# Routed tiles of an attention-and-experts kernel: turning x on TensorE, or by DMA transposes of 16-bit halves that ScalarE weaves together

## What is computed

```python
x = x + xattn(layernorm(x), k, bias, ctx, ctx, 8)   # long convolution, gated by ctx
x = x + ffn(layernorm(x))                           # mixture of experts

scores = softmax(xt @ Wg.T)                         # 16 experts in 4 groups
# the best 2 groups of a token are kept, and in them its best 4 experts
h = silu(einsum('td,eid->eti', xt, W1)) * einsum('td,eid->eti', xt, W3)   # 176 wide
expert_out = einsum('eti,edi->etd', h, W2)
y = einsum('etd,te->td', expert_out, combine)       # weighted sum of a token's experts
z = silu(xt @ Ws1.T) * (xt @ Ws3.T) @ Ws2.T         # shared expert, 352 wide
```

## Time and profile before

| what | value |
|---|---|
| three runs of the program | 396.35, 398.21, 399.11 us; median 398.21 |
| span of the profiled execution, first to last instruction | 395.4 us |
| PE busy | 384.7 us (97%) |
| PEld, DVE, POOL, ACT busy | 279.3, 244.1, 180.3, 162.9 us |
| DMA moved | 83.09 MB in 37,812 packets |

### The profile page before, as it was taken

How to read it: one execution, slowest core, us unless ns; L and a number is a source line. 1 busy time by engine, 2 the same in 40 slices (tenths; PEclk the granted TensorE clock), 3 DMA queues, 4 the chain that set the end, 5 groups by cost and what they waited for, 6 DMA issues and landing times.

```text
span 395.4 us, 9070 instructions
## 1 busy us (share of the span) xinstructions
PE 384.7 (97%) x2146; PEld 279.3 (71%) x2147; DVE 244.1 (62%) x676; ACT 162.9 (41%) x494; POOL 180.3 (46%) x225
## 2 busy tenths in 40 slices
PE   6999999999999999999999999999999999999996
PEld 6788888888888546555667675446767777777765
DVE  3577577987988465788735344443445464646466
ACT  5347656564564362101124333333333333334431
POOL 3254323337888573565553333333333333334333
PEclk9999999999999999999999999999999999999999
DMA  7974474368879996256376873334474737362737
GB/s 248 363 254 139 163 277 144 133 206 278 309 250 335 414 419 258 96 207 223 104 215 219 321 239 107 87 95 134 127 246 136 242 115 242 115 232 103 264 97 251
DMA packets 37812, 83.09 MB, mean 210 GB/s; under 512 B 5930, under 2 KB 25870, under 8 KB 35728
## 3 DMA queue, kind: packets, MB, share of 16 engines
q1 hardware_dynamic: 31248, 64.83, 49.1%
q0 software_dynamic: 6528, 17.84, 11.6%
HBM read 60.21 MB, written 23.48 MB: 212 GB/s over the span
## 4 chain that ended last, share of the span: by engine, by line
PE 79%; DVE 10%; DMA 4%; issue 2%; ACT 2%; SPq 1%; DVEq 1%; POOL 0%; POOLq 0%
PE heads L1382 18%; PE bank L1456 13%; PE heads L1271 11%; PE heads L1424 7%; PE heads L1273 5%; PE bank L1437 5%; PE heads L1392 4%; PE bank L1403 4%; PE bank L1285 3%; DVE kv L734 3%; PE heads L1374 3%; DMA toep<-toep_in 2%; PE bank L1448 2%; DVE prod L763 2%; DMA y_scratch<-toep,dest_i 2%
## 5 line engine op out<-in xcount | busy, mean ns | idle before, releaser
L716 POOL DMA_INDIRECT y_scratch<-toep,dest_i x72 | 71.8, 997 | 112.0 <-DVE dest_i L1131 96.0
L1382 PE MATMUL heads<-experts,toep 128*128 x256 | 86.6, 461 | 0.6 <-DVE toep L1089 0.5
L1271 PE MATMUL heads<-toep,kv 128*128 128x256 f32 x256 | 77.9, 386 | 1.9 <-DVE kv L734 0.8
L661 POOL DMA_INDIRECT rows_scratch<-rows,slot_i x64 | 63.3, 989 | 35.4 <-issue 19.5
L1456 PE MATMUL bank<-experts,toep 88*128 x256 | 66.2, 381 | 1.6 <-DVE toep L1096 1.6
L553 ACT ACTIVATE toep<-heads 128x176 f32<-128x176 f32 x72 | 22.8, 317 | 78.1 <-PE heads L1382 67.2
L1382 PEld LDWEIGHTS heads<-experts,toep 128*128 128x128 f32 x256 | 43.7, 190 | 14.8 <-issue 1.1
L1273 PEld LDWEIGHTS heads<-toep,kv 128*128 128x128 f32 x256 | 48.7, 190 | 6.5
L763 DVE TENSOR_TENSOR prod<-heads,ctx_rep 128x1024 f32<-128x1024 f32 x32 | 39.1, 1221 | 22.3 <-PE bank L1285 19.9
L1096 DVE COPY toep<-heads 88x256 f32<-88x256 f32 x72 | 30.2, 419 | 31.1 <-PE heads L1392 31.1
L1273 PE MATMUL heads<-toep,kv 128*128 128x128 f32 x256 | 49.2, 274 | 0.0
(11 more groups left out here) (240 smaller groups left out, 513.4 us busy)
## 6 DMA issues: line engine op xcount, KB each, us to landing
ctx_rep<-ctxr_in SPq DMA_DIRECT2D x16, 1024.0 KB, 5.0
experts<-experts_in SPq DMA_DIRECT2D x16, 608.0 KB
toep<-rows_scratch SPq DMA_DIRECT2D x56, 144.0 KB
prod<-y_scratch SPq DMA_DIRECT2D x5, 1024.0 KB, 5.5
rows_scratch<-pad_row SPq DMA_DIRECT2D x17, 144.0 KB, 1.8
ctx_tr<-ctxt_in SPq DMA_DIRECT2D x16, 128.0 KB
toep<-toep_in SPq DMA_DIRECT2D x4, 512.0 KB, 7.0
ctx_n<-ctx_in SPq DMA_DIRECT2D x16, 128.0 KB, 2.1
```

The source lines that it names most:

```text
L661: pool.indirect_dma_start(rows_d, bass.IndirectOffsetOnAxis(ap=slot_i[:, u, k:k + 1].bitcast(U32), axis=0), rows[:, u, :], None).then_inc( ...
L716: pool.indirect_dma_start(y_d, bass.IndirectOffsetOnAxis(ap=dest_i[b][:, 0:1].bitcast(U32), axis=0), y_sb[b], None, bounds_check=TOPK * TO ...
L1271: nc.tensor.matmul(y_ps[par][:, i, :], kv[:, q, 0, h * P:(h + 1) * P], toep[:, q * HH + h, :], start=True, stop=False)
L1382: last = nc.tensor.matmul(up_ps[p], x_tr[p][:, blk, :], up_w(e, blk), start=blk == 0, stop=blk == LB - 1)
```

## The change

The turned x no longer comes from TensorE. ACT writes a row in another form: after `norm2` has put the normalised row into a buffer `xn`, a new `split_row(u)` writes its 256 low and its 256 high 16-bit halves one behind the other into the same 1,024 bytes. POOL scatters the same 1,152 bytes a row, as 16-bit elements. SP loads a tile with a transposing DMA of these halves, which lands turned, and loads the last 32 words of each row (128 bytes) by a second, plain DMA. A mixed tile takes two of each. ACT's `src_tr` then weaves low and high halves into words of `x_tr`, two tiles ahead of `up`. SP reads four tiles' addresses with one load into four registers.

```diff
+            def turned(mem, at, lo, count):
+                return sp.dma_start_transpose(in_halves(mem).rearrange("p (r n) -> p r n", n=P)[:, :, lo:lo + count],
+                                              halves_d[bass.ds(at, count), 0:2 * L])
             def gather(t, b, before):
+                if b == 0:
+                    sp.load(row_of, tile_row[0:1, bass.ds(t, DEPTH)])
+                    if is_mixed(t):
+                        sp.load(also_of, other_row[0:1, t - MIXED0:t - MIXED0 + DEPTH])
+                at = sp.snap(row_of[b], min_val=0, max_val=E * REGION)
                 if not (isinstance(t, int) and t < DEPTH):
-                    sp.wait_ge(xtr_ps, t - (DEPTH - 1))
+                    sp.wait_ge(xtr_ready, t - (DEPTH - 1))
                     sp.wait_ge(taken, t - (DEPTH - 1))
-                at = sp.value_load(tile_row[0:1, bass.ds(t, 1)], min_val=0, max_val=E * REGION)
...
                 if is_mixed(t):
-                    sp.dma_start(xg[b][0:HALF], rows_d[bass.ds(at, HALF)]).then_inc(rows_in[b], 16)
-                    also = sp.value_load(other_row[0:1, t - MIXED0:t - MIXED0 + 1], min_val=0, max_val=E * REGION + HALF)
-                    sp.dma_start(xg[b][HALF:P], rows_d[bass.ds(also, HALF)]).then_inc(others_in[b], 16)
+                    turned(xg[b], at, 0, HALF).then_inc(rows_in[b], 16)
+                    also = sp.snap(also_of[b], min_val=0, max_val=E * REGION + HALF)
+                    turned(xg[b], also, HALF, HALF).then_inc(others_in[b], 16)
+                    sp.dma_start(xg[b][0:HALF, L:], rows_d[bass.ds(at, HALF), L:]).then_inc(gates_in[b], 16)
+                    sp.dma_start(xg[b][HALF:P, L:], rows_d[bass.ds(also, HALF), L:]).then_inc(other_gates[b], 16)
                 else:
-                    sp.dma_start(xg[b], rows_d[bass.ds(at, P)]).then_inc(rows_in[b], 16)
+                    turned(xg[b], at, 0, P).then_inc(rows_in[b], 16)
+                    sp.dma_start(xg[b][:, L:], rows_d[bass.ds(at, P), L:]).then_inc(gates_in[b], 16)
...
+            def split_row(u):
+                act.wait_ge(xn_ready, u + 1)
+                nc.scalar.activation(in_halves(rows[:, u, :]).rearrange("p (s l) -> p s l", s=2),
+                                     xn_of(u).bitcast(U16).rearrange("p (l s) -> p s l", s=2), ACT.Copy
+                                     ).then_inc(row_ready, 1)
...
-            def src_tr(w, p):
+            def src_tr(w, p, b, before):
                 if not (isinstance(w, int) and w < 2):
                     act.wait_ge(up_done, w - 1)
-                act.wait_ge(xtr_ps, w + 1)
-                nc.scalar.activation(x_tr[p], xt_ps[p], ACT.Copy).then_inc(xtr_ready, 1)
+                rows_landed(act, w, b, before)
+                nc.scalar.activation(x_tr[p].rearrange("p b n -> p (b n)").bitcast(U16).rearrange("p (n s) -> p n s", s=2),
+                                     in_halves(rows_of(w, b)).rearrange("p (s n) -> p n s", s=2), ACT.Copy
+                                     ).then_inc(xtr_ready, 1)
...
-            def routed_step(t, b, before):
+            def routed_step(w, b, before):
                 p = b % 2
-                silu(t, p)
-                if not (isinstance(t, int) and t == LIVE - 1):
-                    src_tr(t + 1, 1 - p)
-                if not (isinstance(t, int) and t < 2):
-                    store_y(t - 2, p, (b - 2) % DEPTH, before if b >= 2 else before - 1)
+                if not (isinstance(w, int) and w < 2):
+                    silu(w - 2, p)
+                src_tr(w, p, b, before)
+                if not (isinstance(w, int) and w < 4):
+                    store_y(w - 4, p, b, before - 1)
...
                 up(t, p, b)
-                if not (isinstance(t, int) and t == LIVE - 1):
-                    turn_x(t + 1, 1 - p, (b + 1) % DEPTH, before + 1 if b == DEPTH - 1 else before)
```

More of the change, by code:

```diff
@@ L221, in build @@
         s_up, s_silu, s_hid, s_down = sem("shared_up"), sem("shared_silu"), sem("shared_hid"), sem("shared_down")
-        rows_in = [sem(f"rows_in{b}") for b in range(DEPTH)]
-        xtr_ps, xtr_ready, up_done, silu_done, hid_ready, ht_done, htr_ready, dn_done = (
-            sem("xtr_ps"), sem("xtr_ready"), sem("up_done"), sem("silu_done"), sem("hid_ready"), sem("ht_done"),
+        rows_in, gates_in = ([sem(f"{n}_in{b}") for b in range(DEPTH)] for n in ("rows", "gates"))
+        xtr_ready, up_done, silu_done, hid_ready, ht_done, htr_ready, dn_done = (
+            sem("xtr_ready"), sem("up_done"), sem("silu_done"), sem("hid_ready"), sem("ht_done"),
             sem("htr_ready"), sem("dn_done"))
@@ L227, in build @@
         y_sent = [sem(f"y_sent{b}") for b in range(DEPTH)]
-        late_in = [sem(f"late_in{j}") for j in range(LATE)]
+        late_in, late_gates = ([sem(f"{n}{j}") for j in range(LATE)] for n in ("late_in", "late_gates"))
         sends_ready, unit_ps, unit_ready = sem("sends_ready"), sem("unit_ps"), sem("unit_ready")
@@ L232, in build @@
         other_in = [sem(f"other_in{g}") for g in range(MIXED)]
-        others_in = [sem(f"others_in{b}") for b in range(DEPTH)]
+        others_in, other_gates = ([sem(f"{n}{b}") for b in range(DEPTH)] for n in ("others_in", "other_gates"))
         added, finished = sem("added"), sem("finished")
@@ L237, in build, with xn_of @@
         block = ctx.enter_context(nc.Block())
+        def xn_of(u):
+            return spread[:] if u == UNITS - 1 else xn[:]
         def v_forward(q):
@@ L281, in rows_landed, with gates_landed @@
                 eng.wait_ge(rows_in[b], before * 16 + 16)
+            if is_mixed(t):
+                eng.wait_ge(others_in[b], (t - MIXED0) // DEPTH * 16 + 16)
+        def gates_landed(eng, t, b, before):
+            if is_late(t):
+                eng.wait_ge(late_gates[t - LIVE + LATE], 16)
+            else:
+                eng.wait_ge(gates_in[b], before * 16 + 16)
+            if is_mixed(t):
+                eng.wait_ge(other_gates[b], (t - MIXED0) // DEPTH * 16 + 16)
         def is_mixed(t):
@@ L408, in late_gather @@
                 t = LIVE - LATE + j
-                at = sp.value_load(tile_row[0:1, t:t + 1], min_val=0, max_val=E * REGION)
-                sp.dma_start(rows[:, UNITS - LATE + j, :], rows_d[bass.ds(at, P)]).then_inc(late_in[j], 16)
+                if j % DEPTH == 0:
+                    sp.load(late_of, tile_row[0:1, t:t + DEPTH])
+                at = sp.snap(late_of[j % DEPTH], min_val=0, max_val=E * REGION)
+                mem = rows[:, UNITS - LATE + j, :]
+                turned(mem, at, 0, P).then_inc(late_in[j], 16)
+                sp.dma_start(mem[:, L:], rows_d[bass.ds(at, P), L:]).then_inc(late_gates[j], 16)
             others_at = {5: (0,), 7: (1,), 8: (2,), 9: (3,), 10: (4,), 11: (5,), 13: (6,), 14: (7,)}
@@ L581, in _ @@
             copy_xn(UNITS - 1)
+            split_row(UNITS - 2)
             silu_shared(2)
+            split_row(UNITS - 1)
             copy_logits(UNITS - 1)
@@ L1114, in take @@
                 src = rows_of(t, b)
-                rows_landed(dve, t, b, before)
+                gates_landed(dve, t, b, before)
                 if not (isinstance(t, int) and t < DEPTH):
@@ L1303, in transpose_xn @@
                 for blk in range(LB):
-                    last = nc.tensor.transpose(xn_ps[:, blk, :], rows[:, u, blk * P:(blk + 1) * P], ident[:])
+                    last = nc.tensor.transpose(xn_ps[:, blk, :], xn_of(u)[:, blk * P:(blk + 1) * P], ident[:])
                 last.then_inc(xt_done, 1)
@@ L1393, in turn_h @@
                 last.then_inc(ht_done, 1)
-            def turn_x(t, p, b, before):
-                src = rows_of(t, b)
-                rows_landed(pe, t, b, before)
-                if is_mixed(t):
-                    pe.wait_ge(others_in[b], (t - MIXED0) // DEPTH * 16 + 16)
-                if not (isinstance(t, int) and t < 2):
-                    pe.wait_ge(xtr_ready, t - 1)
-                for blk in range(LB):
-                    last = nc.tensor.transpose(xt_ps[p][:, blk, :], src[:, blk * P:(blk + 1) * P], ident[:])
-                last.then_inc(xtr_ps, 1)
             def tile_lists():
@@ L1495, in _ @@
             pe.wait_ge(map_ready, 1)
-            turn_x(0, 0, 0, 0)
             down_shared(UNITS - 2)
```

35 lines of the change are left out of this document (22 added, 13 removed).

## The result

| | time, us (median, runs) | ratio to before, 95% | span of the profiled execution | granted clock |
|---|---|---|---|---|
| before | 397.67 (396.35 to 399.11, 4) | 1 | 395.4 | 1.00 |
| after | 439.41 (438.88 to 441.21, 4) | 1.105 [1.102, 1.108] | 437.6 | 0.965 |

The forecast was 407 with a range of 384 to 426: the side was right and so was the place, the size was not.

A forecast was written before the change was run, and what follows sets the result against it. SP's queue was to replace TensorE as the bound: 27.2 us lost on SP less 18.3 gained from turn_x gives +8.9, so 404.3 on the span and 407 on the median, range 384 to 426.

The forecast's parts named there:

- The place and the mechanism: SP's queue becomes the bound: late loads delay ACT's weave and TensorE's up; SP hardly waits for taken in tiles 16 to 63.
- p: A transposing load's time on SP with its preparation: taken as 1.27 us, bounds 0.43 and 5.1, break-even 1.15.
- SP's price of a tile: SP's work for a plain tile: 1.27 + 0.43 + 0.1 for waits = 1.8 us.
- the eight late loads: Extra loads on SP, four in tiles 24 to 31 and four in 32 to 39, priced at 1.7 us each.
- Address loads: On SP, one load of four addresses, once in four tiles, taken at 0.3 us.
- TensorE's need as predicted: TensorE's pace without turn_x: 2.27 us for a plain tile and 2.54 for a mixed one.
- the 2.0 us of lead: Tiles 8 to 15: loads may run four tiles ahead, of which about 2.0 us is lead, leaving a loss of 1.6.
- The gain: turn_x gone from TensorE's chain: 14.1 us in 64 plain tiles and 4.2 in 8 mixed ones, 18.3 us in all.
- ACT: hidden: ACT's weave takes 0.60 us instead of the copy's 0.38, hidden because it comes two tiles ahead; otherwise 43 us.
- DMA engines: hidden: Transposed tile and gates packets, about 1.0 and 0.3 us of the engines per tile, fit into the pace of 2.4.
- Tiles 0 to 7: First eight tiles on SP: loaded early, so they lose nothing.
- the DMA engines' case: Rival: DMA engines become the bound, 430 us at 2.0 us a tile; chance of 425 and above 0.14.

The follow-up runs named there:

- e8: The changed kernel with each transposing load fetching only the 256 high halves of a row, half the columns and packets: 438.3 us, 1.101 of the kernel before.
- e1: The changed kernel with plain loads of the same bytes in place of the transposing ones, x left unturned: 389.5 us, 0.981 of the kernel before.
- b3: The kernel before, turn_x kept, with each read-back of y rows fetching a quarter of its bytes: 397.1 us, 0.997 of the kernel before.

## Why the prediction was right on the side and wrong on the size

**The place and the mechanism: right.** SP is the bound from the first routed tile to 400 us, ACT's weave waits for a load, up for the weave, and SP no longer waits for `taken`. The one-for-one answer to address loads (36.8 us) shows it.

**p: nearly right.** Taken 1.27 with preparation; measured 1.31 within a mixed pair, 1.37 by itself, and 1.39 up to the gates' load behind it. It came from POOL's row pitch, a different thing; that the two agree is luck, since e8 shows that SP's price does not go by pieces. The Trainium skill's figure for earlier generations ("DMA: Bandwidth & Descriptors", section "Why a DMA increments its semaphore by 16 and not by 1": 631 cycles beside 512) gave an estimate of 0.5 for p, with the full gain as its sum. The trace says 1.20 beside 0.33 us, 3.6 times, and the measurement decides.

**SP's price of a tile: the step that failed most.** The sum took 1.27 + 0.43 + 0.1 for waits = 1.80 us for a plain tile and 3.78 for a mixed one; measured are 2.11 and 4.09, 0.31 more for each. Of that, 0.12 is p, up to the gates' load. The rest, 0.72 instead of 0.53, is the gates' load and the waits behind it. Where a late load follows, which waits for nothing, the gates' load shows alone:

```profile
287.75 0.43 SPq L403 DMA_DIRECT2D toep<-rows_scratch  x1
288.31 1.19 SPq L378 DMA_TRANSPOSE rows<-rows_scratch  x1
```

It takes 0.56 with the next load's preparation, where a "DMA with its preparation" was priced at 0.43; the two waits take 0.15 instead of 0.1. The 0.43 was low for plain loads too: in e1 the same step takes 0.53 (287.91 to 288.44 us). Tiles 8 to 63, with the eight late loads (2.03 on the mean instead of 1.75 for a plain tile and a late one), lose some 19 us more by this.

**Address loads: too cheap.** One load of four was taken at 0.3. Where one stands between a gates' load (289.69, 0.43 long) and the next transposing load (290.83), 0.71 us pass; without one it is 0.29 (350.09 + 0.43 to 350.81). So it takes 0.42 or more, 18 times, some 2 to 3 us.

Stage by stage, from the starts of the first transposing load in each:

| tiles | start to end, us | SP measured | SP predicted | TensorE's need as predicted |
|---|---|---|---|---|
| 8 to 15 | 216.53 to 242.53 | 26.0 | 21.8 | 18.2 |
| 16 to 23, mixed | 242.53 to 277.22 | 34.7 | 31.4 | 20.3 |
| 24 to 31 | 277.22 to 303.95 | 26.7 | 22.1 | 18.2 |
| 32 to 39 | 303.95 to 333.09 | 29.1 | 25.5 | 18.2 |
| 40 to 63 | 333.09 to 400.08 | 67.0 | 57.9 | 54.6 |
| all | | 183.5 | 158.7 | 129.5 |

With the 2.0 us of lead the loss is 183.5 - 129.5 - 2.0 = 52.0 instead of 27.2: 24.8 more, of which the two terms above are 21 to 22. Three gates' loads that took 1.00 to 1.46 us themselves (at 231.27, 254.26 and 302.36), for no reason that the trace shows, are another 2.3; the rest wasn't taken apart.

**The gain: too large, but hardly part of this miss.** 18.3 was predicted from turn_x's pieces on the chain; alone, in the kernel before, it brings 12.4 on the span. "Every piece was on the chain" was true, but the pieces also covered DVE's copy. In the changed kernel that shortfall can count only where TensorE and not SP sets the pace, so it can't be added to SP's loss.

**Tiles 0 to 7: not nothing.** The starts of up of tiles 0, 8 and 64, before and after:

```profile
198.60 1.35 PE L1382 MATMUL heads<-experts,toep 128*128 x4
219.18 1.35 PE L1382 MATMUL heads<-experts,toep 128*128 x4
365.01 1.35 PE L1382 MATMUL heads<-experts,toep 128*128 x4
```

```profile
199.42 1.35 PE L1436 MATMUL heads<-experts,toep 128*128 x4
222.66 1.35 PE L1436 MATMUL heads<-experts,toep 128*128 x4
408.50 1.35 PE L1436 MATMUL heads<-experts,toep 128*128 x4
```

On the span 437.6 - 404.3 = 33.3 us are missing. From tile 8 to 64 the kernel takes 185.84 us instead of 145.83, 40.0 more, where the prediction's terms give 27.2 - 14.7 = 12.5 (14.7 is the part of the gain of 48 plain and 8 mixed tiles): 27.5 of the 33.3, most of it the 24.8 of SP above. Tiles 0 to 7 were priced at nothing on SP, with 1.8 of gain; they take 23.24 us instead of 20.58, 4.4 off. SP is late there already: 21.4 us lie between its loads of tiles 0 and 8 (195.16 and 216.53), and TensorE needs 18.2. The first up starts 0.8 later, which is about as much as in b3 (199.26), where only the read-back differs. From tile 64 to the end 1.3 of 1.8 us of gain come.

**ACT: hidden, as said.** The weave takes 0.68 (0.60 predicted). **DMA engines: hidden, as said**; half the transposed bytes change nothing. Landing is 2.7 us in the median where 2.5 was expected.

**The range.** It left out 426 and above as the DMA engines' case. The same side was reached with p as forecast, since the sum multiplied every small price on SP by 56 to 72 and gave them no range: 0.31 more per tile, over 64 tiles, weighs as much as the whole gain.

## What to carry to other kernels

Before work is moved into DMA descriptors, price every instruction of the issuing queue per tile, the small second load most carefully, and compare that sum with the pace of the bound engine; SP waited 31.8 us for `taken` in total, and the change asked more of it than that. A load that is split in two (rows and gates) pays for a second instruction on its queue, here 0.56 of the 2.11 us of a tile, and in the sizes tried here a transposing load costs nearly one price, so it wants to be large and few. And work that is taken off the bound engine's chain may have been covering another engine's latency: measure the removal alone, in a kernel that leaves the work out, before adding what its replacement costs.

## What the runs showed of the hardware

- A transposing DMA with a register address takes SP 1.17 to 1.25 us in 71 of the 80 loads of the kernel after. It is nearly the same for 64 rows (1.17) and 128 (1.20), and for 256 columns of 16-bit halves (1.18) and 512; a plain one of the same bytes takes 0.33.
- A plain DMA of 128-byte rows that follows a transposing one takes SP 0.43 instead of 0.33, but with the preparation of a load that waits for nothing only 0.56 instead of the 0.53 of the run with plain loads.
- Landing hardly differs: 2.7 us in the median transposed, 2.3 plain. The Trainium skill, "Advanced Engine Details and Errata", section "X-Bar Transpose (TRN2)", says that transposing DMAs are as fast as regular ones; the landing nearly agrees, the issuing queue's time (1.20 beside 0.33) does not.
- The granted clock fell to 0.83 and 0.80 on the mean of a 20 us stretch, part of it at the lower level of 1.2 GHz, where TensorE was busy for 15 to 16 us of it, and to 0.95 in one of 36 us with 25.7; it stood at 1.00 in a stretch of 20 us with 19.4.
